# Gate scores in four column tiles, batch 0 split amid the norm, routing moved into batch 0

## What is computed

```python
xn = layernorm(x)
# attention: windows of 128 at a stride of 64; 16 heads of 16; only the first 512 output rows of each batch are kept
q, k, v = split(xn @ w_qkv + b_qkv)
attn = softmax(q_w @ k_w.T / 4) @ v_w @ w_out + b_out
# mixture of 8 experts, the best 2 of each row
scores = xn @ gate_w.T                    # 4096 rows x 8 experts
top, idx = top_k(scores, 2); p = softmax(top)
ffn = sum_k p[k] * (silu(h1) * h2) @ w3[idx[k]].T      # h1, h2 = xn @ w12[idx[k]].T
out = x + attn + ffn
```

## Time and profile before

| what | us |
|---|---|
| median of 3 executions | 770.64 (769.15 to 770.73) |
| the profiled execution | 768.43 |
| its span (first to last instruction) | 766.5 |
| TensorE busy | 688.3 (90%) |
| VectorE busy | 574.2 (75%) |
| ScalarE busy | 492.4 (64%) |
| GpSimd busy | 318.7 (42%) |

### The profile page before, as it was taken

One profiled execution on the slowest core, in us unless ns is written; L12 is line 12 of the kernel. 1 busy time (PEld: TensorE's weight loads), 2 busy tenths in 40 slices (PEclk: granted clock), 3 DMA queues, 4 the chain that ended last, 5 costly groups with the idle time before them and its releaser, 6 DMA issues.

```text
span 766.5 us, 17138 instructions
## 1 busy us (share of the span) xinstructions
PE 688.3 (90%) x5632; PEld 541.8 (71%) x5633; DVE 574.2 (75%) x911; ACT 492.4 (64%) x838; POOL 318.7 (42%) x359
## 2 busy tenths in 40 slices
PE   0998587797999999999999999999989998989984
PEld 0877465585887888777877878787767676766763
DVE  4862788986787777877777777777758779797883
ACT  4321264456667676676766767676657788978884
POOL 2000259521444454444544445444410144566653
PEclk9985898897999999999999999999999999999998
DMA  8789074363111111111111111111127777875830
GB/s 281 269 308 272 18 186 178 101 217 131 42 54 48 48 55 41 55 49 48 53 42 53 50 48 52 44 49 52 49 69 215 206 222 205 273 202 178 217 123 28
DMA packets 66175, 92.56 MB, mean 121 GB/s; under 512 B 6256, under 2 KB 53232, under 8 KB 66128
## 3 DMA queue, kind: packets, MB, share of 16 engines
q1 hardware_dynamic: 56096, 65.68, 28.9%
q0 software_dynamic: 6864, 18.75, 7.7%
q10 hardware_dynamic: 3168, 7.48, 2.8%
HBM read 59.06 MB, written 32.83 MB: 120 GB/s over the span
## 4 chain that ended last, share of the span: by engine, by line
PE 68%; DVE 9%; ACT 7%; issue 6%; POOL 4%; DMA 3%; SPq 1%; DVEq 0%; ACTq 0%; POOLq 0%
PE PS L1157 61%; PE PS L1384 4%; DVE SMALL L863 3%; ACT WORK L727 3%; PE PS L1362 2%; DVE XN L1028 2%; POOL XN L577 2%; DMA XN<-in_x 2%; POOL OTS L585 1%; ACT QS L722 1%; DVE WORK L943 1%; DMA xt_scratch<-WALL 1%; PE PS L1180 1%; POOL WALL L577 1%; DVE WORK L936 1%
## 5 line engine op out<-in xcount | busy, mean ns | idle before, releaser
L336 DVE TENSOR_TENSOR WS<-WALL,WS 128x1024 fp32r<-128x1024 f32 x144 | 176.4, 1226 | 89.3 <-ACT WS L789 88.2
L1157 PE MATMUL PS<-WS,XTS 128*128 128x512 f32 x852 | 235.6, 412 | 1.9 <-DVE XTS L857 1.5
L1157 PEld LDWEIGHTS PS<-WS,XTS 128*128 128x128 f32 x852 | 151.1, 190 | 46.1 <-DVE XTS L857 14.0
L789 ACT ACTIVATE WS<-WALL 128x1024 fp32r x144 | 152.2, 1058 | 38.8 <-issue 36.0
L1157 PE MATMUL PS<-WALL,WORK 128*128 x568 | 136.2, 383 | 0.8 <-ACT WORK L805 0.8
L1157 PEld LDWEIGHTS PS<-WALL,WORK 128*128 128x128 f32 x568 | 102.2, 190 | 12.9 <-issue 1.0
L618 POOL DMA_INDIRECT WORK<-xn_scratch,WORK x72 | 100.9, 1401 | 24.8 <-issue 21.6
L622 POOL DMA_INDIRECT ys_scratch<-SIDE,WORK x36 | 41.9, 1163 | 117.8 <-ACT SIDE L815 117.8
L863 DVE TENSOR_REDUCE SMALL<-PS 128x8 f32<-128x1024 f32 x64 | 77.4, 1210 | 9.3 <-PE PS L1157 9.2
L727 ACT ACTIVATE WORK<-PS 128x512 f32<-128x512 f32 x128 | 69.4, 594 | 21.4 <-PE PS L1157 18.3
L585 POOL TENSOR_TENSOR OTS<-SIDE,XN 128x256 f32<-128x256 f32 x32 | 25.1, 785 | 132.0 <-DVE XN L1028 67.6
(11 more groups left out here) (124 smaller groups left out, 1076.6 us busy)
## 6 DMA issues: line engine op xcount, KB each, us to landing
WALL<-ys_scratch SPq DMA_DIRECT2D x16, 512.0 KB, 6.9
parts_scratch<-WORK SPq DMA_DIRECT2D x32, 240.0 KB, 2.4
QS<-parts_scratch SPq DMA_DIRECT2D x16, 480.0 KB, 4.9
WALL<-in_wexp ACTq DMA_DIRECT2D x16, 384.0 KB, 5.6
WALL<-in_wexp SPq DMA_DIRECT2D x16, 384.0 KB, 7.0
XN<-in_x SPq DMA_DIRECT2D x4, 1024.0 KB, 13.0
xn_scratch<-XN SPq DMA_DIRECT2D x4, 1024.0 KB, 6.7
WALL<-in_x SPq DMA_DIRECT2D x8, 512.0 KB, 5.8
```

The costliest lines, as they stand in the source:

```text
L336: eng.tensor_tensor(out=WS[:, 1 - k, half, 1], in0=weights, in1=WS[:, 1 - k, half, 0].bitcast(F32), op=ALU.subtract).then_inc(low_ready[ha ...
L789: act.activation(WS[:, 1 - k, half, 0], weights, ACT.Copy).then_inc(high_ready[half], 1)
L1157: return pe.matmul(o, a, b, start=start, stop=stop)
```

## The change

**Gate scores.** `score_pair` goes. The gate weights are now padded with zeros to 32 columns (GW of 128x32 per chunk) and are the stationary operand; the turned tokens stream. `gates(b)` makes 8 matmuls for a whole batch, each tile of 128 tokens in its own column tile (partitions 32j to 32j+31 of PSUM), ACT copies the 128x128 result (`take_gates`), and one matmul by columns of the identity turns it (`turn_gates`).

**Homes.** Each batch's turned tokens have a place: three own buffers, two in the probabilities' buffer, two in the second half of QS; only batch 7 shares one, with batch 3, and waits for its store.

**Batch 0 earlier.** Queries, keys and values of batch 0 are projected after pair 1, not after pair 8 and at the end. ACT copies the values, in place of the DVE. The DVE splits between `variance(2)` and `normalise(2)`. SP writes and reads the stacks before most stores of tokens.

**Routing.** `route(0)` lies behind the third `take_max`, `route(1)` in unit 0 of batch 0, ranks and bases in unit 2, experts of tiles and shares in unit 3; the tags begin one unit later, with two in unit 7. POOL's `find_slots` lies behind `divide(0)`. POOL makes 40 places (14, 14 and 12), DVE 24.

The diff, cut to its core:

```diff
-PLACES_POOL = 48
+PLACES_POOL = (0, 0, 14, 28, 40)
...
-        XT = temp(NC_D * 3 * L).rearrange("p (c n) -> p c n", c=NC_D)
-        GW = temp(NC_D * E).rearrange("p (c e) -> p c e", c=NC_D)
+        XT_HOME = [temp(NC_D * L) for _ in range(3)]
+        GW = temp(NC_D * GROUP).rearrange("p (c e) -> p c e", c=NC_D)
+        GTS = temp(2 * P).rearrange("p (b n) -> p b n", b=2)
...
+        XT = [v.rearrange("p (c n) -> p c n", c=NC_D)
+              for v in (XT_HOME[0], probs[:, 0:n // 2], probs[:, n // 2:n], XT_HOME[1], XT_HOME[2],
+                        spare[:, 0:n // 2], spare[:, n // 2:n], XT_HOME[1])]
@@ SP @@
             store_xn(0)
             store_xt(1)
             store_xn(1)
-            store_xt(2)
-            store_xt(3)
-            store_xn(2)
-            store_xn(3)
-            store_xt(4)
+            outs(0, 0)
+            outs(0, 1)
+            store_xt(2)
+            backs(0, 0, 0)
+            backs(0, 0, 1)
+            store_xt(3)
...
+            sp.wait_ge(xt_out[1], 16)
             load_tokens(0, True)
+            store_xn(2)
+            for src in range(4, B - 1):
+                store_xt(src)
+            store_xn(3)
+            store_xt(B - 1)
+            for src in range(2, B):
+                sp.wait_ge(xt_out[src], 16)
@@ ACT @@
             for i in range(NT // 2):
-                if i % 3 == 0 and 1 <= i // 3 <= EARLY:
+                if i % 2 == 1 and i >= NT // 2 - 2 * EARLY:
                     act.wait_ge(x_in[3], 16)
-                    load_expert(i // 3 - 1)
+                    load_expert((i - NT // 2 + 2 * EARLY) // 2)
+                b = 2 * i // TB
                 act.wait_ge(tok_full, i + 1)
-                if i >= 6 and i % 2 == 0:
-                    act.wait_ge(scored, i - 2)
-                    act.wait_ge(xt_out[(i // 2) % 2], 16 * ((i // 2 - 1) // 2))
+                if b == B - 1:
+                    act.wait_ge(xt_out[3], 16)
+                    act.wait_ge(scored, 4)
...
-                if i in (3, 7):
-                    take_sqrt((i + 1) // 4 + 1)
-                if i == FIRST_STEP:
+                if i == 1:
                     act.wait_ge(consts_in, 80)
                     for n, blk in enumerate(BLOCKS):
                         take_part(blk, FIRST_BANK[blk], first_full, n + 1)
+                    for n in range(NWIN):
+                        take_values(n, FIRST_VALUES[n // 2][:, n % 2 * D:(n % 2 + 1) * D], (first_full, 6 + n // 2 * 2),
+                                    values_taken)
+                if i in (3, 11):
+                    take_sqrt(i // 8 + 2)
+                if i % 2 == 0 and i >= 4:
+                    take_gates(i // 2 - 2)
+            take_gates(B - 2)
+            take_gates(B - 1)
@@ PE @@
+            def gates(b):
+                pe.wait_ge(tok_free, 2 * b + 2)
+                if b == 0:
+                    pe.wait_ge(values_taken, NWIN)
+                for ch in range(NC_D):
+                    for j in range(TB):
+                        last = mm(GT_BANK[j * GROUP:(j + 1) * GROUP, b % 2, :], GW[:, ch, :],
+                                  XT[b][:, ch, j * P:(j + 1) * P], ch == 0, ch == NC_D - 1)
+                last.then_inc(gates_full, 1)
+            def turn_gates(b):
+                pe.wait_ge(gates_taken, b + 1)
+                to = G_BANK.rearrange("p (b j e) -> p b j e", b=B, j=TB)[:, b]
+                mm(to, GTS[:, b % 2, :], IDF[:].rearrange("p (j e) -> p j e", j=TB)[:, :, 0:E]).then_inc(scored, 1)
+            for i in range(NT // 2):
                 turn_pair(i)
-                score_pair(i - 1)
-                if i == FIRST_STEP:
+                if i == 1:
...
+                    pe.wait_ge(tok_free, 2)
                     for blk in BLOCKS:
+                        project_block(FIRST_BANK[blk][:, 0:SPAN], blk, XT[0], first_full)
+                    for n in range(NWIN):
+                        project_values(FIRST_VALUES[n // 2][:, n % 2 * D:(n % 2 + 1) * D], n, XT[0], first_full)
+                if i % 2 == 1 and i >= 5:
+                    turn_gates(i // 2 - 2)
+                if i % 2 == 1 and i >= 3:
+                    gates(i // 2 - 1)
+            turn_gates(B - 2)
+            gates(B - 1)
...
+            turn_gates(B - 1)
@@ DVE @@
+            variance(0)
+            variance(1)
+            normalise(0)
...
+            normalise(1)
+            variance(2)
             for n in range(4):
                 split(n, True)
-            route(0)
-            route(1)
+            normalise(2)
+            variance(3)
+            normalise(3)
...
-                    if first == 0 and u >= 3:
+                    if first == 0:
+                        if u == 0:
+                            route(1)
+                        if u == 2:
+                            take_ranks()
+                            bases()
                         if u == 3:
+                            experts_of_tiles()
+                            shares()
+                        if u == 4:
                             dve.wait_ge(tiles_ready, 2)
-                        tags(u - 3)
+                        if u >= 4:
+                            tags(u - 4)
+                        if u == UNITS - 1:
+                            tags(4)
@@ POOL @@
-            for w in range(3):
+            divide(0)
+            find_slots()
+            for w in range(1, 4):
                 divide(w)
                 make_places(w)
```

More of the change, by code:

```diff
@@ L11 @@
 from contextlib import ExitStack
-from functools import partial
 import concourse.bass as bass
@@ L378, in out_, with backs @@
                         sp.dma_start(to[:, 0:NPART, :], PARTS[:, :, blk, :]).then_inc(parts_out[blk], 16)
-                def back(blk):
-                    half = blk % 2
+            def backs(nb, par, half):
+                for blk in BLOCKS[2 * half:2 * half + 2]:
                     of = pd_dram[nb, blk // 2, half].rearrange("l (d h) t -> (l d) (h t)", h=HH)
@@ L391, in back @@
                                          ).then_inc(stack_in[par][half], 16)
-                for half in range(2):
-                    for n in (2 * half, 2 * half + 1):
-                        sp.wait_ge(parts_ready, nb * 4 + n + 1)
-                        out_(BLOCKS[n])
-                    if at_once and half:
-                        store_xt(5)
-                    if not at_once or half:
-                        for n in range(0 if at_once else 2 * half, 2 * half + 2):
-                            back(BLOCKS[n])
-            stacks(0, 0, at_once=True)
+            store_xn(0)
+            store_xt(1)
+            store_xn(1)
+            outs(0, 0)
[4 more added lines that the diff above has]
+            store_xt(3)
             def load_tokens(b, first=False):
@@ L446, in begin @@
                     sp.wait_ge(probs_ready, 2 * UNITS * b + 2)
-                stacks(b + 1, (b + 1) % 2)
+                for half in range(2):
+                    outs(b + 1, half)
+                    backs(b + 1, (b + 1) % 2, half)
             def send(b):
@@ new lines, in bases @@
+            def bases():
+                inc = INC.rearrange("p (e t) -> p e t", e=E)
+                link(tt(CMP, inc[:, :, NT - 1:NT].to_broadcast([P, E, NT]),
+                        TH.unsqueeze(1).to_broadcast([P, E, NT]), ALU.is_gt))
+                link(red(NTL, CMP, ALU.add))
+                link(dve.tensor_tensor_scan(out=INCT, data0=ONE8, data1=NTL, initial=0.0, op0=ALU.mult, op1=ALU.add))
+                link(tt(BASE, INCT, NTL, ALU.subtract))
+                link(ts(BASE, BASE, float(P), None, ALU.mult, ALU.bypass))
+                dve.sem_inc(bases_ready, 1)
@@ new lines, in experts_of_tiles, with shares @@
+            def experts_of_tiles():
+                link(tt(CMPJ, INCT.unsqueeze(1).to_broadcast([P, XS_TILES, E]), wide(JI), ALU.is_le))
+                link(red(EJF, CMPJ, ALU.add))
+                link(ts(EJF, EJF, float(E - 1), None, ALU.min, ALU.bypass))
+                link(dve.tensor_copy(EJ, EJF[0:1, :]))
+                dve.sem_inc(temps_done, 1)
+            def shares():
+                dve.wait_ge(e2_ready, 1)
+                link(ts(M1, E2, 1.0, None, ALU.add, ALU.bypass))
+                link(dve.reciprocal(out=M2, in_=M1))
+                link(ts(PW[:, 0, :], M2, 0.5, None, ALU.mult, ALU.bypass))
+                link(dve.scalar_tensor_tensor(out=PW[:, 1, :], in0=E2, scalar=0.5, in1=M2, op0=ALU.mult,
+                                              op1=ALU.mult))
@@ L1331, in batch @@
                         shift_row()
-                    if first == 1 and u == 2:
+                    if first == 0 and u == 1:
+                        ranks()
+                    if first == 0 and u == 3:
+                        pe.wait_ge(ranks_taken, 1)
+                    if first == 1 and u == MAP_UNIT:
                         slot_map()
-                    if first == 1 and u == 3:
```

(1 more changed line is left out.)

220 lines of the change are left out of this document (93 added, 127 removed).

## The result

| | before | after |
|---|---|---|
| median, us | 770.37 (768.96 to 772.46, 11 executions) | 773.19 (771.04 to 775.09, 11 executions) |
| the profiled execution, us | 768.43 | 773.47 |
| span, us | 766.5 | 771.7 |
| first scores of batch 0 (T) | 80.71 | 77.29 |
| first split of batch 0 (S) | 94.36 | 88.97 |

The ratio after to before is 1.0032, with a 95% interval of 1.0018 to 1.0046: the change costs 0.3%. The prediction was 761.9 us (753 to 770), and faster with a chance of 0.86. It was wrong in size and in sign.

The account below looks back on a forecast made before the run. It took PE and late stores to bound the norm stage, then the DVE to the map. 61.5 + 12.2 + 70.6 + 4.5 put the map at 148.8, not 157.5: 8.7 less, 759.7 profiled, plus 2.2 is 761.9 us (753 to 770).

Parts of the forecast that it names:

- Start of the norm stage: Batch 0's projections on PE at the norm stage's start: blocks end at 30.0 us, values at 33.8, at full clock.
- Seven steps of two pairs: Norm stage, pairs 2 to 15: 3.0 us of PE work a step, replacing 4.9, with the clock falling.
- Rival 4: Column tiles of the gate matmuls do not run side by side: 9.7 us slower, 780.3 us; chance 0.05.
- The loads on ACT: Late norm stage: four load issues hold ACT 1.8 us; two such groups put copy 11 at 49.5 us.
- SP: SP's norm-stage queue: stacks land by about 53 us, batch 3's store after 6.8 us at 53.5; nothing charged.
- rival 2: PE keeps full clock over turns and gates: T at 58, waits 3 us, 756.9 us in all; chance 0.15.
- From T to S: First scores to first split of batch 0: maxima and route(0) take 12.2 us, before 13.65; table load hidden.
- Batch 0 and the map: First split to the map's end: 70.6 us of DVE work plus 4.5 of waits.
- the bound I gave: Batch 0 to the map: no wait of PE over 2 us behind POOL's places.
- The sum: Map taken at 148.8 us against 157.5, 8.7 less; profiled execution 759.7, median 2.2 above it, 761.9.
- the fifth: Batch 0 waits for tokens or stacks behind SP's stores; T stays at 70 or later: 770.6 us; chance 0.03.
- Rival 1: Norm stage ends late from slow load issues and batch 3's late store: T about 67, 767.4 us; chance 0.20.

Follow-up runs that it names:

- late_loads: The changed kernel with the loads of experts 0 to 3 moved from ACT's queue to SP, behind the norm stage's stores of tokens: 758.79 us.
- home0: The changed kernel with batch 7's turned tokens in batch 0's home, so copy 14 waits for no store; expert loads stay on ACT: 768.20 us.
- both: The changed kernel with the edits of late_loads and home0 together: 754.88 us, ratio 0.9819 to the kernel before.
- early_stacks: The kernel of both, with SP writing parts and reading stacks ahead of some stores, and the last group's root at copy 8: 748.89 us.
- last_loads: early_stacks with route(0) before the first scores, route(1) behind the third maximum, and expert loads moved behind batch 1's parts and stacks on SP: 757.93 us.

## Why the prediction was wrong

By its own steps, with the profile of the kernel after:

- *Start of the norm stage*: blocks to 30.0, values to 33.8. Measured 30.5 and 33.95. Right.
- *Seven steps of two pairs* at 3.0 us. Measured 2.42 for the first three, with the clock at full, 0.6 us a step better; then 3.56, with ACT held by issues, and 6.57, with PE waiting 3.38 us for `normalise(3)`. The 3.0 rested on the clock falling "once the work is narrow, as it did after 48 us", but the same trace of before has 1.00 from 26 to 41 us over the same transposes and 8-column records, with PE busy throughout; the reason was wrong. The `gates` are 0.64 to 0.65 us at full clock and 1.08 at half. Rival 4 (column tiles not side by side) is dead, and a step took no longer than its rows. By the Trainium skill's rule on changes of the tiling mode (TensorEngine Tiling (Array Packing), Key Properties) a drain would have come on top; the trace shows none.
- *The loads on ACT*: copy 11 foreseen at 49.5, measured 47.08, since the steps were faster. The issues were costed at 1.8 us for four; they took 3.0, 3.0, 1.9 and 1.9, and copy 11 is at 44.29 without them (late_loads). That was too low and did no harm: in home0, with all issues on ACT, PE is through with the norm stage at 59.8, ahead of the foreseen 61.5. What the loads do to other transfers was not costed at all.
- ***SP***: **this is the step that failed.** It said that the stacks land by about 53, that the store of batch 3 is issued then and lands 6.8 us later, and "Nothing is charged". The second half of the parts landed at 58.0, where the step had the reads behind it issued by 46.5; the store was issued at 59.26, not 46.5, and took 11.0 us, so that copy 14 lay at 70.68 and not behind a landing at 53.5. T was 77.29 and not 61.5: 15.8 us. I took landing times from the kernel before, and in the same text moved 6.3 MB of loads into the very stretch in which these transfers run. A smaller error sits in the same step: an issue was set at 0.55 us, and the eight issues of parts took 8.9 us in the kernel after and 8.1 in late_loads, so that without the loads too the reads are out at 49.8 and not at 46.5. Taking the loads out gives 12.0 of the 15.8 us (late_loads), freeing the home another 6.9 (both): T at 58.4, the value of rival 2.
- *From T to S*: 12.2 foreseen, 11.7 measured. The table load was hidden, as costed. Right.
- *Batch 0 and the map*: 75.1 foreseen (70.6 of work, 4.5 of waits), 74.3 measured, with waits of 2.1 and 1.5 us. Right (all named waits of the DVE come to 4.9), also in that PE's waits behind places shrank: two of 0.8 and 1.0 us, and one of 2.4 that is over the bound I gave.
- *The sum*: the map was to end at 148.8 and ended at 163.3. The 14.5 us are the 15.8 of T less 0.5 and 0.8 of the next two steps. The median missed by only 11.3, and part of that is luck: 2.2 us were added from the profiled execution to the median, as before, but the one of the kernel after lies 0.3 over its median.

Of the rivals, the fifth described what came (batch 0 waits for tokens and stacks, since SP's transfers queue), and the stated condition for being wrong, T past 70, was met. It had a chance of 0.03 and a price of 770.6, which is 2.6 short: that is the time of the kernel before, and about what the sum gives for a T of 70, the least that it could be. Rival 1 named the same two causes, slow loads in a full queue and a late store, and allowed 5.5 us for both; they cost 15.8. Its reason against, "the queues are emptier until 44 us than before", was true, and should have been read the other way round: what is taken from the time before 44 us is put into the time after. Rivals 1 and 5 were one mechanism at two prices, and its upper price was never worked out.

The change itself then is sound: with the loads elsewhere and a free home it is 7.4 us faster than the kernel before with its loads elsewhere. early_stacks, at 748.89 us and 0.9729 (0.9705 to 0.9753), beats both kernels, by 2.7% and some 3%.

## What to carry to other kernels

When a change moves bulk loads, list which small transfers are in flight in the stretch that they move into, above all a write and a read back that the next stage waits for, and price these at a landing time measured beside such loads (here 11 to 15.6 us instead of 3 to 9), not at that of the old trace. A queue that waits for a landing passes its delay on to all that stands behind it (here the store of batch 3 was issued 9.4 us later for it), so two waits that seem independent (stacks and a store) end together, and removing one shows little. A load that isn't needed for 100 us can stand elsewhere. Of the four places tried here, amid the parts and stacks of batch 0 cost 13 us against the one behind the norm stage (home0 and both), ahead of batch 2's tokens 9 (last_loads), and the gap before the parts at most 2: try three places before judging the rest of the change.

## What was not expected of the hardware

- The clock stayed at full through narrow work: windows of the kernel after from 26 to 47 us show 1.00, in the last two of them with PE busy 4.17 of 5.0 us and then 3.42 of 6.0, and fell behind that (0.66 from 47 to 53 us), where the copies were late and PE waited more; in the idle stretch it is at half.
- An issue of a load is not the cost of a load: four issues held ACT 1.9 to 3.0 us (1.8 to 3.0 before), while the same loads added 9 to 10 us to the reads of the stacks on another queue, and 4 us to the writes of parts (medians, after against late_loads).
- The length of an issue depends on what the queue has before it: three issues of parts took 1.44 us on SP in early_stacks, ahead of the store of the second normalised rows, and 3.40 behind it in late_loads.
- The DMA engines' busy share hides this: from 41 to 66 us it is 1.00 or more in the kernel after and 0.96 to 1.08 in late_loads, at 239 to 391 and 237 to 387 GB/s. The kernel before had 1.08 as well from 54 to 66 us, with reads of KS of 6.9 us. What differs is whose bytes they move. The windows of the kernel after (stretch, length, busy us of PE, PEld, DVE, ACT and POOL, granted clock, DMA share, GB/s):

```profile
41.00:47.00 6.00, 3.42 (x47) 2.26 (x45) 2.02 (x11) 1.93 (x5) 0.00 (x0) 1.00 1.00 287
47.00:53.00 6.00, 3.35 (x26) 2.67 (x26) 3.56 (x13) 1.73 (x5) 0.00 (x0) 0.66 1.05 391
...
60.00:66.00 6.00, 0.00 (x0) 0.00 (x0) 0.00 (x0) 0.00 (x0) 0.00 (x0) 0.50 1.03 239
```
